# Inverting the row sums of attention in 16 columns, with VectorE transposes around it, in place of a copy and four 128-column inversions

## The reference

```python
att = einsum('bhtd,bhsd->bhts', q, k) / sqrt(D)          # H = 16, D = 32, T = 2048
att = where(tril & (column % 4 != 3), att, -inf)         # every fourth key is masked out
y   = softmax(att, -1) @ v
x = x + layernorm(attention(layernorm(x)) @ Wp + bp)
idx = argmax(log_softmax(logits) + gumbel(u))            # one of 8 weights
x = x + layernorm(layernorm(x) @ W[idx] + b[idx])
```

## Time and profile before

| what | us |
|---|---|
| median of 3 runs | 2775.3 |
| lowest, highest | 2772.9, 2775.33 |
| the profiled execution | 2770.63 |
| its span, first to last instruction | 2768.8 |
| TensorE busy in it | 2555.6 |
| VectorE busy | 1972.0 |
| ScalarE busy | 1615.7 |
| GpSimd busy | 1484.0 |

### The profile page before, as it was taken

The page is one execution under the profiler, slowest core; times in us unless marked ns, Lnnn a source line. Parts: engine busy times, 40 slices in busy tenths (PEclk is TensorE's granted clock), DMA queues, the critical chain, the costliest instruction groups (busy, mean ns, idle before and its releaser), DMA issues.

```text
span 2768.8 us, 46168 instructions
## 1 busy us (share of the span) xinstructions
PE 2555.6 (92%) x17416; PEld 1014.9 (37%) x17416; DVE 1972.0 (71%) x4199; ACT 1615.7 (58%) x2781; POOL 1484.0 (54%) x1350
## 2 busy tenths in 40 slices
PE   1999999999999999999999999999999999999985
PEld 0444333333343433333344433333334343333222
DVE  8667876876587687787566778678647767677623
ACT  4556656666655566566665555666665565655662
POOL 2335465665546366376653547467455635546563
PEclk7999999999999999999999999999999999999997
DMA  4211110010021111001011211101002110100000
GB/s 130 76 33 55 36 46 21 22 41 16 25 64 54 39 37 48 15 26 40 11 50 48 63 37 45 33 14 41 11 21 68 50 33 25 51 16 18 20 1 19
DMA packets 89192, 103.98 MB, mean 38 GB/s; under 512 B 11562, under 2 KB 61578, under 8 KB 88970
## 3 DMA queue, kind: packets, MB, share of 16 engines
q1 hardware_dynamic: 88970, 101.04, 12.3%
HBM read 39.59 MB, written 16.78 MB: 20 GB/s over the span
## 4 chain that ended last, share of the span: by engine, by line
PE 64%; DVE 22%; ACT 5%; POOL 4%; issue 3%; DMA 1%; SPq 1%; POOLq 0%; ACTq 0%; DVEq 0%
PE psO L1045 13%; PE psM L1004 11%; PE psS L1028 10%; DVE MP L807 9%; PE psU L1061 8%; PE psW L981 7%; PE psW L982 6%; PE psW L983 6%; ACT P L710 3%; DVE SC L826 2%; DVE STA L773 2%; DVE XR L785 2%; PE psS L1031 1%; DVE XP L793 1%; PE psM L1007 1%
## 5 line engine op out<-in xcount | busy, mean ns | idle before, releaser
L710 ACT ACTIVATE P<-psS,EX 128x512 f32<-128x512 f32 (+2 forms) x1920 | 1122.0, 631 | 668.3 <-PE psS L1028 357.4
L807 DVE TENSOR_REDUCE MP<-psM 128x1 f32<-128x512 f32 (+8 forms) x2112 | 1107.8, 560 | 502.1 <-PE psM L1004 269.0
L581 POOL TENSOR_TENSOR P<-P 128x512 f32<-128x512 f32 x576 | 725.5, 1288 | 119.6 <-ACT P L710 118.9
L1004 PE MATMUL psM<-KST,QST 96*128 96x512 f16 (+8 forms) x2112 | 640.0, 335 | 59.1 <-DVE MP L807 47.2
L1028 PE MATMUL psS<-QST,KST 98*128 98x512 f16 (+2 forms) x1920 | 618.9, 357 | 29.5 <-ACT P L710 22.3
L1045 PE MATMUL psO<-P,V 128*32 128x512 f32 (+2 forms) x3840 | 463.2, 554 | 10.6 <-ACT P L710 8.9
L586 POOL TENSOR_TENSOR SC<-SC 128x512 f32<-128x512 f32 x64 | 83.7, 1307 | 554.9 <-DVE SC L826 554.9
L1004 PEld LDWEIGHTS psM<-KST,QST 96*128 96x128 f16 x2112 | 200.8, 97 | 466.6 <-DVE MP L807 272.4
L1028 PEld LDWEIGHTS psS<-QST,KST 98*128 98x128 f16 x1920 | 171.1, 97 | 405.2 <-issue 190.0
L1061 PE MATMUL psU<-P,ONES 128*32 128x512 f32 (+2 forms) x2688 | 299.3, 517 | 0.0
L826 DVE RECIPROCAL SC<-SC 128x128 f32<-128x128 f32 x256 | 231.7, 929 | 79.5 <-ACT SC L718 79.5
(11 more groups left out here) (129 smaller groups left out, 3152.7 us busy)
## 6 DMA issues: line engine op xcount, KB each, us to landing
XB<-in_L_attn_x_dram SPq DMA_DIRECT2D x64, 256.0 KB, 2.7
XR<-in_L_attn_x_dram SPq DMA_DIRECT2D x64, 256.0 KB, 2.7
QST<-QKH SPq DMA_DIRECT2D x128, 128.0 KB, 3.2
out_dram<-XR SPq DMA_DIRECT2D x64, 256.0 KB, 2.0
KST<-QKH SPq DMA_DIRECT2D x128, 96.0 KB, 2.6
QST<-QKL SPq DMA_DIRECT2D x64, 128.0 KB, 3.3
KST<-QKL SPq DMA_DIRECT2D x64, 96.0 KB, 2.7
QST<-MROW SPq DMA_DIRECT2D x128, 4.0 KB
```

What stands on the lines that cost most here:

```text
L581: e.tensor_tensor(P[:, acc, a, :], P[:, acc, a, :], P[:, buf, a, :], ALU.add).then_inc(g_s, 1)
L710: e.activation(P[:, p_buf[u, g, sb_], a, t0:512], psS[:, s_slot[step] % 2, t0:512], ACT.Exp, scale=EX[:, 1:2]).then_inc(a_e, 1)
L807: e.tensor_reduce(MP[:, j, r, a, ci:ci + 1], psM[:, m_slot[s] % 2, 0:n], AX.X, ALU.max).then_inc(v_m, 1)
L1004: i = e.matmul(psM[:, k, 0:n], QST[0:96, h, 128 * r:128 * r + 128], KST[0:96, h, c0:c0 + n], start=True, stop=not last)
```

## The change

The row sums leave psU through VectorE instead of ScalarE. VectorE's transpose works within squares of 32x32. Since the 32 rows of a head in psU are equal, after a transpose of all 16 squares of a row of squares every column of a square holds the sums of 32 queries, one query to a partition. One column of each square, 16 in all, is enough: it goes through one reciprocal into the new tile RS (128 x 16). A second transpose, which reads each of the 16 columns 32 times over, gives back the layout of before in SC[:, 0].

"out" is now the copy of psO alone and no longer waits for the sum. "invert" is one step of three instructions with a wait between them; it waits for the last sum and for "scale" of the group before. The next group's sum waits for the first of the three instead of for "out". In the planner "out" costs 570 ns instead of 1050, "invert" is one step of 1600 ns due at s + 0.95 instead of four of 850 ns due from s + 1.1 on. All five lists are planned anew from this.

```diff
-            before = free
+            before = [("dve", "invert", *divmod(s - 1, 4))] if s else []
...
-            add("act", s + 0.95, 1050, ("out", u, g), [("pe", "pv", u, g, last), ("pe", "sum", u, g, last)],
-                [("SC", ("gp", "olow", u, g))])
-            for i in range(4):
-                add("dve", s + 1.1 + 0.02 * i, 850, ("invert", u, g, i), [("act", "out", u, g)])
-            add("gp", s + 1.1, 1225, ("scale", u, g), [("dve", "invert", u, g, i) for i in range(4)])
+            add("act", s + 0.95, 570, ("out", u, g), [("pe", "pv", u, g, last)], [("SC", ("gp", "olow", u, g))])
+            add("dve", s + 0.95, 1600, ("invert", u, g), [("pe", "sum", u, g, last)]
+                + [("gp", "scale", *divmod(s - 1, 4))] * (s > 0))
+            add("gp", s + 1.1, 1225, ("scale", u, g), [("dve", "invert", u, g), ("act", "out", u, g)])
...
+        RS = sb("RS", [128, 16], F32)
...
                 elif kind == "out":
                     u, g = s[1:]
                     n = 4 * u + g
-                    ac.wait_ge(p_u, PE["sum", u, g, 3 * (u % NJ) + 2])
                     if n:
                         ac.wait_ge(g_o, GP["olow", *divmod(n - 1, 4)])
-                    e.activation(SC[:, 0, :], psU[:, :], ACT.Copy).then_inc(a_o, 1)
                     ac.wait_ge(p_pv, PE["pv", u, g, 3 * (u % NJ) + 2])
                     e.activation(SC[:, 1, :], psO[:, :], ACT.Copy, scale=SS[:, 2:3]).then_inc(a_o, 1)
...
                 elif kind == "invert":
-                    u, g, i = s[1:]
-                    c = slice(128 * i, 128 * i + 128)
-                    dv.wait_ge(a_o, AC["out", u, g] - 1)
-                    e.reciprocal(SC[:, 0, c], SC[:, 0, c]).then_inc(v_o, 1)
+                    u, g = s[1:]
+                    n, at = 4 * u + g, DV[s] - 3
+                    dv.wait_ge(p_u, PE["sum", u, g, 3 * (u % NJ) + 2])
+                    if n:
+                        dv.wait_ge(g_o, GP["scale", *divmod(n - 1, 4)])
+                    e.transpose(SC[:, 0, :], psU[:, :]).then_inc(v_o, 1)
+                    dv.wait_ge(v_o, at + 1)
+                    e.reciprocal(RS[:, :], SC[:, 0, :].rearrange("p (b c) -> p b c", c=32)[:, :, 0]).then_inc(v_o, 1)
+                    dv.wait_ge(v_o, at + 2)
+                    e.transpose(SC[:, 0, :], RS[:, :].rearrange("p (b o) -> p b o", o=1).broadcast_to([128, 16, 32])
+                                ).then_inc(v_o, 1)
...
                     if n:
-                        pe.wait_ge(a_o, AC["out", *divmod(n - 1, 4)])
+                        pe.wait_ge(v_o, DV["invert", *divmod(n - 1, 4)] - 2)
```

More of the change, by code:

```diff
@@ L420, in sandwich_block @@
                                             "whigh": ("w", 16 if s[0] == "whigh" and s[1] < 2 else 1), "exp": ("e", 1),
-                                            "out": ("o", 2), "ohigh": ("o", 1), "shift": ("m", 1),
+                                            "out": ("o", 1), "ohigh": ("o", 1), "shift": ("m", 1),
                                             "unturn": ("t", 2 if s[0] == "unturn" and s[1] == 1 else 1)}[s[0]]))
@@ L426, in sandwich_block @@
             "fold": ("f", 18 if s[-1] else 1), "stats": ("ln", 4), "norm": ("n", 1), "cast": ("n", 1),
-            "high": ("q", 1), "peak": ("m", 1), "peaks": ("m", 3), "invert": ("o", 1)}[s[0]])
+            "high": ("q", 1), "peak": ("m", 1), "peaks": ("m", 3), "invert": ("o", 3)}[s[0]])
         GP = counted(order.gp, lambda s: {
@@ L583, in _ @@
                     u, g = s[1:]
-                    gp.wait_ge(v_o, max(DV["invert", u, g, i] for i in range(4)))
+                    gp.wait_ge(v_o, DV["invert", u, g])
                     gp.wait_ge(a_o, AC["out", u, g])
```

## The result

The changed kernel takes 2776.3 us, median of 12 runs, against 2773.6 for the kernel before, median of 12 runs on the same chips. The ratio is 1.0017, with an interval of 1.0009 to 1.0025: 4.7 us slower, which lies within what was called the same (0.2%). The forecast was 2759 and faster. Each ratio is good to about 0.0015 either way (4 us), so a difference of two is good to about 6 us.

A forecast was written before the change was run, and what follows sets the result against it. TensorE was taken to bound one long stage that repeatedly meets VectorE, with latency ruling the short end. Terms -2.3 - 18 - 1 + 5 = -16 us from 2770.6 gave 2754.3, 2759 on the median's scale; range 2728 to 2783.

The forecast's parts named there:

- Sizes of the new steps: VectorE per head group: transposes 0.68 us each, small reciprocal 0.25, gaps 0.08; 1.69 us in place of 3.72.
- The rival of the dear transpose: Transposes run at the reciprocal's rate, block 7.7 us; +79 us, 2854; chance 0.03.
- (a): Program end: the block starts where the copy did and ends at 2710.5 instead of 2712.8; minus 2.3 us.
- (b): Long stage: cheaper reciprocals take at most 36 us off the chain of waits; half taken, minus 18 us.
- the 55% of the term: Share (2.03/3.72) of the long stage's 65.8 us of reciprocals on the chain that the change removes: 36 us at most.
- (c): ScalarE's copy of psU, 38.2 us busy, goes; worth up to 3.3 us on the chain, 1 us taken.
- (d): The wait for the last row sum moves from ScalarE to VectorE; net 17 us more standing, costing 5 us.
- no price of its own in this trace: All five engine queues may be dealt differently by the planner; nothing charged, only both ends of the range widened.
- The rival: The uncut block lets no maxima pass while psM has two buffers; 55 us lost against 38 gained, +17, 2792; chance 0.12.
- half of 110 us: Over 63 groups the uncut block holds 110 us longer; half reaching TensorE loses 55 us.
- TensorE takes it all over: TensorE itself is next late at each meeting; only the end's 2.3 us stay, 2773; chance 0.17.
- VectorE down 130 us and the time by less than 5: Sign in the profile after that TensorE took over: VectorE falls by 130 us, the time by under 5 us.

The follow-up runs named there:

- e1: Kernel before, every order and ScalarE's copy kept; transpose, 16-column reciprocal and transpose back stand in the places of the first three reciprocals; 2755.9 us, ratio 0.9941.
- e6: e1 with the first transpose reading psU itself, ScalarE's copy of psU gone and the next sum waiting for that transpose; 2751.5 us, ratio 0.9910.
- e9: Every instruction and wait of the changed kernel, uncut block too, in the order of the kernel before, at the first reciprocal's place; 2763.7 us, ratio 0.9962.
- e11: Changed kernel with the block cut into three planner steps, a planner rule grouping TensorE's float32 steps, and truer costs of three VectorE step kinds; 2732.1 us, ratio 0.9850.
- e13: Changed kernel, block uncut, no new rule, with truer planner costs for VectorE's normalising and casts alone; 2743.5 us, ratio 0.9883.
- e14: Changed kernel with the block cut into three planner steps and truer VectorE planner costs, no rule for float32 steps; 2739.1 us, ratio 0.9860.
- e17: Kernel before with truer planner costs for VectorE's normalising and casts and nothing else; 2754.4 us, ratio 0.9938.
- e3: Changed kernel's orders, with four 128-column reciprocals straight from psU in one step instead of transpose, reciprocal, transpose; 2877.2 us, ratio 1.0374.
- e15: Kernel before, its copy and four reciprocals kept, with the planner rule grouping TensorE's float32 steps and truer VectorE costs; 2737.2 us, ratio 0.9869.

## Why the prediction was wrong, step by step

*Sizes of the new steps.* Right: 0.71, 0.25 and 0.71 us with gaps of 0.03, 1.75 in all, for 1.69 forecast. The rival of the dear transpose is out. An estimate from the 311 ns that the Trainium skill gives for a 128x128 transpose of 2-byte data ("VectorE: DVE Perf Modes", "The three transpose paths"), four times as many columns, would be 1.24 us; the rows have 0.71. The Trainium skill, "Vector Engine (DVE) Microarchitecture Reference", section 3.8, has the transpose pipelined at one element per cycle and lane; nothing in the rows speaks against it, but with one width only they don't show a rate.

*(a), the end.* Right: 2.27 us less standing for 2.3 forecast.

*(b), half of the 36 us on the chain.* Right in size: e1, which holds 1.6 us of (a) too (TensorE stands 5.73 us at the end), is 16.4 us faster where this and (b) make 19.6, within the 6 us of the comparison. The way there was another than the 55% of the term: in e1 the block has 0.2% of the chain, so nearly all 66 us of the reciprocals left it and a quarter was gained. In the changed kernel it has 1.6%, not the 1.1% forecast. That reading the reciprocals off the chain and taking half works is seen only where nothing else is altered.

*(c) and (d), copy gone and wait moved.* The amount of the wait was right (43.0 us in 32 cases for 46 forecast), but the price of the two terms together had the wrong sign: e6 against e1 is -8.6 us where -1 + 5 = +4 was forecast. The difference is near the limit of what these ratios tell, but a cost of 4 us is ruled out by it; which of the two terms was off is not shown, since e6 changes both. In the old order VectorE waits 30.7 us for the sum where it waited 28.7 for the copy, so nothing was added there.

*What the sum left out.* The step that failed is the sentence that the replanned orders have "no price of its own in this trace", and with it that the one-piece block stood at nothing in the sum and only in a rival. Measured, the piece costs 14 to 20 us and the new order, as it was dealt for the change, 10 to 15; two other deals put it at 5 and at nothing. The forecast allowed 10 us for an unlucky deal, in its upper bound only. The rival had the piece's mechanism right, place and buffers, as the rows of e6 and e9 show; its price, half of 110 us, was about three times too high, and its bill lacked the order. The sign that the prediction named for it, open idle behind the maxima over 47.2 us, came true (50.5). Without these two terms the forecast was -16; with e6's -25 as the relief, 14 for the piece and 15 for the order (or 20 and 10) against it, the sum is +4.7.

*The rivals.* "TensorE takes it all over" would have given nearly the right number for the wrong reason: e1 and e6 show that the relief counts in the old order, and the chain after has TensorE at 65%, not more. The signs named for it, VectorE down 130 us and the time by less than 5, came near being met (VectorE's steps 124 us less, its total 91, the time up 4.7); they can't tell "taken over" from "eaten by something else". Only undoing parts could.

*Why the new order was worse.* Shown: for the same instructions the order of the change was, by 15 us (e9); three deals lie 15 us apart, and the best of them is no worse than the old order; in the profiled executions of e9 and the changed kernel the difference is busy time of TensorE at a lower mean clock, not standing; and with VectorE costs nearer the trace the same kernel gains 37 us by ratios, the kernel before 14 to 17. Not shown: which single spot carries the difference, and what lowers the clock. The spot at 1650 us, a cast stretched to 1.38 us, 1.20 us of standing and 5 us and more at half clock, is one instance. How much is the truer costs and how much is luck of the deal in a single pair can't be settled either; that all four kernels with the truer costs and a counterpart without them lie below it (e11, e13, e14, e17) speaks for the costs. But 7 to 10 us of each of these gains are there at about 200 us already, with the start of the program; that the stretched casts of the long stage were what made the orders fragile is argued, not shown.

## What to carry to other kernels

Where an order is planned from costs, a cheaper instruction is two changes: the instruction, and a new order that inherits every error of the other costs. Price the second by running the old instructions' order with the new instruction first, and correct the planner's costs from the profile before judging the change. Compare TensorE's busy time for the same instructions as well as its waits: an order can cost time in the clock with no more standing. And what a step costs others goes by the length of the piece in which nothing else of its engine can pass: with two buffers of 0.7 us each ahead of it, one piece of 1.7 us gave back more than half of what 2 us less work a group had won.

## What the runs showed of the hardware

In the changed kernel VectorE's transpose of 128x512 float32 takes 714 ns in the mean out of PSUM (704 to 719) and 711 within SBUF (711 to 714), the latter from a source that repeats each element 32 times, and the 16-column reciprocal with a step of 32 takes 253 (702, 704 and 246 ns in e1, where both transposes are within SBUF). A reciprocal of 128 columns takes 929 ns within SBUF and 909 out of PSUM (e3).

Casts on VectorE get stretched beside GpSimd steps. Counted over the changed kernel, the 61 casts of 128x512 from float32 to float16 with no GpSimd step beside them take 411 to 429 ns; the 131 others take 386 to 1509. It is not any GpSimd step: 17 casts beside one of a single column (RR) stay at 410 to 427 ns, 23 that began beside one of the additions of 128x512 in P take 698 to 1509. Normalising behaves alike (72 steps alone, 534 to 549 ns; the others up to 1519). The transposes did not show this, 704 to 719 ns alone and 704 to 718 in the 30 cases beside a GpSimd step. The Trainium skill, "GPSIMD Engine Reference", section "1. Specifications", says that GpSimd shares its SBUF interfaces with VectorE and that VectorE's 2-port modes contend for them; the rows agree with it as far as casts and normalising go, though no run here took a GpSimd step away.

TensorE's granted clock is 0.50 in the window from 1651 us, behind a standing of 1.20 us, 1.00 in the one from 1640 and again in the one from 1658. No run had it otherwise at that spot. Over a whole kernel executions of the same lists differ in their mean clock, and the time goes with it: e15 took 2735.95 us at 0.990 and 2748.49 at 0.984, e14 2733.1 at 0.991 and 2742.9 at 0.987, which is 2 to 2.5 us for each 0.001. Over the 7 thousandths between the medians of e9 and of the changed kernel (0.985 and 0.978) that would be 14 us and more, an estimate beside the 15 measured. Which comes first, the slower clock or the standing behind it, these pairs don't tell.
